# Another head for a fused attention and feed-forward kernel: inputs in another order, the first batch by pairs of tiles, the second from a transposed copy

## The reference

```
xn  = layernorm(x)                              # over the last axis, no gain and no offset
q   = xn @ wq.T + bq;  k = xn @ wk.T + bk;  v = xn @ wv.T + bv
p   = softmax(q @ k.T / 16)                     # 1024 x 1024 for each batch
low = up_aux @ (lora_up @ (lora_down @ down_aux))
out = x + p @ v  +  xn @ (W + low).T + ffn_b
```

## Time and profile before

| What | Value |
|---|---|
| Median of three runs | 518.73 us |
| The profiled execution, its own time | 518.57 us |
| Its span, first to last instruction | 516.8 us |
| Granted TensorE clock over the span | 1.000 |
| PE busy | 506.3 us, 98% of the span |
| DVE, POOL, ACT busy | 367.4, 373.7, 276.6 us |

### The profile page before, as it was taken

How to read it: one execution, slowest core, us unless ns; L and a number is a source line. 1 busy time by engine, 2 the same in 40 slices (tenths; PEclk the granted TensorE clock), 3 DMA queues, 4 the chain that set the end, 5 groups by cost and what they waited for, 6 DMA issues and landing times.

```text
span 516.8 us, 8100 instructions
## 1 busy us (share of the span) xinstructions
PE 506.3 (98%) x2948; PEld 448.6 (87%) x2948; DVE 367.4 (71%) x839; ACT 276.6 (54%) x589; POOL 373.7 (72%) x221
## 2 busy tenths in 40 slices
PE   5999999999999999999999999999999999999997
PEld 4677897989989898898989989898998989899897
DVE  4789866867589584885868767696758748376594
ACT  3746667365744747267381655736474462724450
POOL 2834785986789966999669979699678976671730
PEclk9999999999999999999999999999999999999999
DMA  8020004000040003200050100501002010000001
GB/s 238 39 82 0 1 33 173 1 41 2 26 179 1 41 1 109 96 2 41 1 197 8 42 2 0 204 1 42 0 35 90 1 42 1 41 1 2 41 9 74
DMA packets 8694, 25.04 MB, mean 48 GB/s; under 512 B 1850, under 2 KB 3792, under 8 KB 7760
## 3 DMA queue, kind: packets, MB, share of 16 engines
q1 hardware_dynamic: 7328, 24.38, 13.0%
q10 hardware_dynamic: 1328, 0.16, 0.2%
HBM read 16.15 MB, written 8.39 MB: 47 GB/s over the span
## 4 chain that ended last, share of the span: by engine, by line
PE 94%; DVE 1%; ACT 1%; issue 0%; DVEq 0%
PE o_ps L1078 12%; PE o_ps L1080 12%; PE o_ps L1079 12%; PE g_ps L998 10%; PE g_ps L1000 10%; PE g_ps L999 10%; PE s_ps L998 8%; PE s_ps L999 8%; PE s_ps L1000 8%; PE o_ps L998 1%; PE o_ps L999 1%; PE o_ps L1000 1%; ACT prod L607 1%; PE s_ps L1078 0%; PE s_ps L1080 0%
## 5 line engine op out<-in xcount | busy, mean ns | idle before, releaser
L507 POOL TENSOR_TENSOR p_lo<-s,p_hi 128x1024 fp32r<-128x1024 f32 x60 | 144.3, 2439 | 40.0 <-ACT p_hi L657 40.0
L650 ACT ACTIVATE s<-s,e 128x512 f32<-128x512 f32 x128 | 84.3, 714 | 116.3 <-DVE s L848 116.3
L1078 PE MATMUL o_ps<-v_hi,p_hi 128*128 128x258 f32 x480 | 136.5, 284 | 0.0
L1080 PE MATMUL o_ps<-v_hi,p_lo 128*128 128x258 f32 x480 | 136.0, 283 | 0.0
L1079 PE MATMUL o_ps<-v_lo,p_hi 128*128 128x256 f32 x480 | 135.8, 283 | 0.0
L1079 PEld LDWEIGHTS o_ps<-v_lo,p_hi 128*128 128x128 f32 x480 | 91.5, 191 | 1.6
L1078 PEld LDWEIGHTS o_ps<-v_hi,p_hi 128*128 128x128 f32 x480 | 90.2, 188 | 1.6
L1080 PEld LDWEIGHTS o_ps<-v_hi,p_lo 128*128 128x128 f32 x480 | 91.2, 190 | 0.0
L807 DVE SCALAR_TENSOR_TENSOR tile_max<-s_ps,e,tile_max 128x512 f32<-128x512 f32 x80 | 59.9, 748 | 32.9 <-PE s_ps L1000 30.7
L998 PE MATMUL s_ps<-xt_hi,zt_hi 128*128 128x512 f32 x192 | 75.0, 390 | 0.0
L999 PE MATMUL s_ps<-xt_lo,zt_hi 128*128 128x512 f32 x192 | 74.7, 389 | 0.0
(11 more groups left out here) (157 smaller groups left out, 988.8 us busy)
## 6 DMA issues: line engine op xcount, KB each, us to landing
out<-base SPq DMA_DIRECT2D x15, 512.0 KB, 2.7
x_sb<-in_L_attn_x SPq DMA_DIRECT2D x7, 1024.0 KB, 7.8
x_t<-in_x_t SPq DMA_DIRECT2D x6, 1024.0 KB, 5.8
x_sb<-in_L_attn_x SPq DMA_DIRECT2D x4, 256.0 KB, 6.7
out<-base SPq DMA_DIRECT2D x4, 128.0 KB, 1.9
s<-in_L_attn_wk SPq DMA_DIRECT2D x1, 256.0 KB, 3.1
s<-in_L_attn_wq SPq DMA_DIRECT2D x1, 256.0 KB, 6.2
s<-in_L_attn_wv SPq DMA_DIRECT2D x1, 256.0 KB, 6.9
```

Source lines behind the costliest of these rows:

```text
L507: nc.gpsimd.tensor_tensor(p_pair(g, p_lo_sb, j), s_pair(j), p_pair(g, p_hi_sb, j).bitcast(f32), ALU.subtract).then_inc(p_lo_made, 1)
L650: nc.scalar.activation(s[:, n, :], s[:, n, :], ACT.Exp, bias=e[b % 2][:, n:n + 1]).then_inc(p_made, 1)
L1078: nc.tensor.matmul(o[:, 0:D + ONES], hi, v_hi[i][:, n, 0:D + ONES], start=first, stop=False)
L1080: mm = nc.tensor.matmul(o[:, 0:D + ONES], lo, v_hi[i][:, n, 0:D + ONES], start=False, stop=last)
```

## The change

- Loads: x's first piece goes ahead of wk, wq and wv go ahead of the third and fourth piece. The small columns (bq, bk, lora_down, lora_up) come in one array `small` that the host packs, by one DMA.
- PE order in the head: LoRA, the row for e and the bias columns; then the transposes by pairs of tiles (`turn`), between them A by plain float32 matmuls (`make_a`, no split of wk and wq); then V of the first four tiles (`first_v`, 256 columns), two of z, the other transposes, the first score tile, V of tiles 4 and 5, the second score tile, the other two of z, the other six score tiles, the feed-forward of all tiles (`first_ffn`, 256 columns), and V of tiles 6 and 7.
- Batch 1 uses the transposed copy (`EARLY = 1`): its 16 transposes, `make_xn(1)` and its first `make_prod` go; `load_t(1)`, `make_stat_cols(1)`, two `make_stat_row`, `norm_x_t(1, ...)`, `make_xt_hi` and `make_xt_lo` are added in the head. Its z groups move to places 1 and 2.
- DVE: two of the four `prod` products of batch 0 go from POOL to DVE (`make_late_prod`); `vf_lo` (two subtractions) goes from POOL to DVE; the bn_stats of batch 2 go from the head into the score maxima of chunk 1.

The core of the diff, with the new functions:

```diff
+        TURN_BANKS = (g_ps[0], g_ps[1], g_ps[1], s_ps[3])
+        FIRST_V_BANKS = (o_ps[0], g_ps[0], o_ps[0], o_ps[0])
+        FIRST_Z_BANKS = (s_ps[0], s_ps[1], o_ps[0], o_ps[1])
+        FIRST_FFN_BANKS = (o_ps[0], o_ps[1], o_ps[0], o_ps[1])
...
-        FIRST = [{0: (0, 1), 1: (2, 3), 2: (4, 5), 3: (6, 7)}, V_GROUPS]
-        LATER = [{1: (4, 5), 2: (6, 7)}, V_GROUPS]
+        PLACES = [{1: (0, 1), 2: (2, 3)}, V_GROUPS]
...
             load(1)
+            load_t(1)
             load(2)
...
# POOL
             make_x_bias(0)
...
+            norm_x_t(1, 0)
+            norm_x_t(1, 1)
+            make_xt_lo(1, 0)
             shift_raw(0)
...
# ACT
+            make_raw(0, 1)
             act.wait_ge(ffn_summed, 1)
             nc.scalar.activation(vf_hi[:, :, D:2 * D], ffn_t_sb, ACT.Copy).then_inc(ffn_hi_made, 1)
+            make_stat_cols(1)
+            make_xt_hi(1, 0)
             make_p(0, 0)
             make_p(0, 1)
+            first_v_hi(3)
             make_p_hi(0, 0)
...
             make_p_hi(0, 1)
+            make_xt_hi(1, 1)
             make_p(0, 4)
             make_p(0, 5)
             make_raw(1, 0)
...
# DVE
+            first_z_lo(0)
+            make_late_prod(2)
+            make_late_prod(3)
+            first_z_lo(1)
+            turned_lo(2)
+            turned_lo(3)
...
             nc.vector.tensor_tensor(ffn_t_sb, two(o_ps[1][:, :]), ffn_t_sb, ALU.add).then_inc(ffn_summed, 1)
+            dve.wait_ge(x_loaded[1], DMA)
+            make_stats(1, range(0, 4))
             make_tile_max(0, 0)
+            first_v_lo(2)
+            make_stats(1, range(4, TILES))
+            make_mean_var(1)
             make_tile_max(0, 1)
+            first_z_lo(2)
+            first_z_lo(3)
+            dve.wait_ge(ffn_hi_made, 1)
+            nc.vector.tensor_tensor(vf_lo[:, :, D:2 * D], ffn_t_sb, vf_hi[:, :, D:2 * D].bitcast(f32),
+                                    ALU.subtract).then_inc(ffn_lo_made, 1)
             make_tile_max(0, 2)
             make_tile_max(0, 3)
+            make_stat_row(1, 0)
+            make_tile_max(0, 4)
+            make_stat_row(1, 1)
+            make_tile_max(0, 5)
             nc.vector.tensor_reduce(e_row_sum[:, :], e_row, AXIS, ALU.add).then_inc(e_row_sum_made, 1)
+            make_tile_max(0, 6)
+            make_tile_max(0, 7)
 
             make_max_t(0)
             make_block_max(0)
+            add_first_ffn(0)
             make_max_col(0)
             spread_max_col(0)
+            add_first_ffn(1)
             make_top(0)
             shift(0, 0)
             shift(0, 1)
             shift(0, 2)
+            add_first_ffn(2)
+            shift(0, 3)
...
# PE
+            def first_v(j):
+                pe.wait_ge(turned_lo_made, j + 1)
...
+                elif j == 3:
+                    pe.wait_ge(first_ffn_added, 3)
+                first_tokens(FIRST_V_BANKS[j], j, slice(0, D)).then_inc(first_v_mm, 1)
+
+            def first_ffn(j):
...
+                elif j > 1:
+                    pe.wait_ge(first_ffn_added, j - 1)
+                first_tokens(FIRST_FFN_BANKS[j], j, slice(D, 2 * D)).then_inc(first_ffn_mm, 1)
...
+            pe.wait_ge(small_loaded, DMA)
+            pe.wait_ge(lora_loaded, 2 * DMA)
+            nc.tensor.matmul(o_ps[0][0:RANK, 0:D], lora_down_t, down_aux_sb,
+                             start=True, stop=True).then_inc(low_rank_mm, 1)
             pe.wait_ge(bq_spread, DT)
             pe.wait_ge(wk_loaded, DMA)
...
+            turn(0)
+            make_a(0)
+            turn(1)
+            make_a(1).then_inc(a_mm, 1)
+            first_v(0)
+            first_v(1)
+            first_z(0)
+            first_z(1)
+            turn(2)
+            turn(3)
...
+            scores(0, 0)
+            first_v(2)
+            scores(0, 1)
+            first_z(2)
+            first_z(3)
+            for n in range(2, TILES):
                 scores(0, n)
...
+            for j in range(PAIRS):
+                first_ffn(j)
+            first_v(3)
```

More of the change, by code:

```diff
@@ L274, in two, with pair, group_bank, rstd_count @@
             return ap.rearrange("p (t n) -> p t n", t=DT)
[L276 to L283, removed]
-            return g_ps[k % 2]
[L286 to L296, removed]
+        def pair(ap):
+            return ap.rearrange("p (m n) -> p m n", m=2)
+        TURN_BANKS = (g_ps[0], g_ps[1], g_ps[1], s_ps[3])
+        FIRST_V_BANKS = (o_ps[0], g_ps[0], o_ps[0], o_ps[0])
+        FIRST_Z_BANKS = (s_ps[0], s_ps[1], o_ps[0], o_ps[1])
+        FIRST_FFN_BANKS = (o_ps[0], o_ps[1], o_ps[0], o_ps[1])
+        POOL_PRODS = 2
+        def group_bank(k):
+            return g_ps[k % 2]
+        def rstd_count(b):
+            return len(STAGES) + b
+        def stage_of(tile):
+            return [first <= tile < end for first, end in STAGES].index(True)
+        def prods(b):
+            return PAIRS * b + POOL_PRODS
+        def pair_of_columns(j):
+            return slice(2 * j * PT, (2 * j + 2) * PT)
         LAST = CHUNKS * B - 1
@@ L348, in _, with load_first @@
         def _(sp):
-            sp.dma_start(wk_sb, rows(wk)).then_inc(wk_loaded, DMA)
-            for j in range(4):
+            def load_first(j):
                 n = TILES // 4
@@ L567, in _ @@
         def _(act):
[L568 to L572, removed]
+            act.dma_start(small[:, :], small_in).then_inc(small_loaded, DMA)
@@ new lines, in turned_hi, with first_v_hi, make_z_hi @@
+            def turned_hi(j):
+                act.wait_ge(turned_mm, j + 1)
+                nc.scalar.activation(xt_hi[0][:, :, pair_of_columns(j)], two(TURN_BANKS[j][:, :]), ACT.Copy)\
+                  .then_inc(turned_hi_made, 1)
+            def first_v_hi(j):
+                act.wait_ge(first_v_mm, j + 1)
+                nc.scalar.activation(v_hi[0][:, 2 * j:2 * j + 2, 0:D], pair(FIRST_V_BANKS[j][:, :]), ACT.Copy)\
+                  .then_inc(first_v_hi_made, 1)
+            def make_z_hi(ps, h, d):
+                return nc.scalar.activation(zt_hi[:, d, half(h)], ps[:, :], ACT.Identity, bias=z_bias[:, d:d + 1])
@@ L664, in _ @@
+            make_xn(0)
+            act.wait_ge(wv_loaded, DMA)
+            nc.scalar.activation(vf_hi[:, :, 0:D], wv_t_sb, ACT.Copy).then_inc(wv_hi_made, 1)
+            act.wait_ge(mid_rank_mm, 1)
+            nc.scalar.activation(mid_rank, o_ps[0][0:UDIM, D:2 * D], ACT.Copy).then_inc(mid_rank_made, 1)
+            turned_hi(0)
+            make_xn(2)
+            turned_hi(1)
             act.wait_ge(a_mm, 1)
             nc.scalar.activation(a_hi[:, :, :], two(s_ps[2][:, :]), ACT.Copy, scale=SCALE).then_inc(a_hi_made, 1)
-            for k in range(DT):
-                make_group_hi(0, k)
@@ L893, in _ @@
               .then_inc(b_parts_made, 1)
-            make_first_xn(DVE_XN[1:])
+            dve.wait_ge(wv_hi_made, 1)
+            nc.vector.tensor_tensor(vf_lo[:, :, 0:D], wv_t_sb, vf_hi[:, :, 0:D].bitcast(f32), ALU.subtract)\
+              .then_inc(wv_lo_made, 1)
+            turned_lo(0)
+            make_first_xn(3)
+            for j in range(2, 4):
+                dve.wait_ge(x0_loaded[j], DMA)
+                make_stats(0, range(2 * j, 2 * j + 2))
+            turned_lo(1)
+            make_mean_var(0, range(4, TILES))
             dve.wait_ge(a_hi_made, 1)
@@ L935, in _ @@
[L935 to L939 removed]
+            add_first_ffn(2)
+            shift(0, 3)
+            shift(0, 4)
+            shift(0, 5)
+            add_first_ffn(3)
+            first_v_lo(3)
             for g in range(LAST):
```

490 lines of the change are left out of this document (245 added, 245 removed).

## The result

The changed kernel takes 523.98 us (median of 4, 523.51 to 524.38) against 518.59 in the same measurement: ratio 1.0101, 95% interval 1.0089 to 1.0113, so 5.4 us slower where 4.0 were forecast. The profiled execution took 524.38 us, its span is 522.3, 5.5 more than before.

What follows compares the result with a forecast made beforehand. PE was taken to bound loop and head, DVE's head work to decide the change: +4.7 us at the start of chunk 2's scores, -0.7 for a vanished later wait, so 518.57 + 4.0 = 522.6 us; range 519.2 to 526.0.

Steps and rivals of the forecast that it cites:

- The loads: Start of head: LoRA loads gate PE's first matmul, at 5.1 us; bounds move the end by -0.5 and +2.7.
- The clock: Head: PE's clock rises from 1.2 to 2.4 GHz at 14 us; bounds 9 and 18 move the mark -1.5, +1.9.
- DVE's list: Head, from z_lo(0) to last score maximum: 19.4 us of DVE work plus waits, ending at 43.1; the deciding term.
- Maximum to third add: Behind chunk 0's scores: 7.55 us of dependent DVE work; PE waits 3.0, 0.5, 1.6; chunk 1's scores +4.8.
- Rival 3: PE's gap from 42.5 us: clock falls to the lower level, some 4 us more, 526.6 us; chance 0.07.
- Chunk 1 to the mark: From chunk 1's scores to chunk 2's scores (the mark): P times V at 64.7, mark at 82.2, +4.7 us.
- The wait for raw: Chunk 1's eighth score tile: PE waits for ACT's raw(1, 1), 1.6 us with restart.
- the 0.54 stall: PE's wait for DVE at 86.34 us goes, with its restart: -0.7 us.
- POOL "costs nothing": POOL's added 12.2 us lies in idle time, done at 55 before ACT wants it at 60: no cost.
- Rival 1: Head: DVE keeps up, last maximum before 39.1, PE wins 9.0 us, kernel gets faster, 513.6 us; chance 0.08.

Runs made afterwards that it cites:

- e5: Changed kernel with the two low-rank (LoRA) matmuls moved behind the first transpose pair and A's first half: 522.57 us.
- e10: Changed kernel with 27 matmuls of zeros on PE ahead of the wait for the first loads: 520.02 us.
- e9: e8 and e5 together on the changed kernel: 519.36 us, in two groups, 518.14 to 518.79 and 519.93 to 520.87.
- e13: The kernel of e9 run again unchanged, for a trace: times in the same two groups, profiled execution 520.85 us.
- e7: Changed kernel with the parts of e2, and batch 1's statistics earlier on DVE and ACT: 521.77 us.
- e3: Changed kernel without batch 1's row statistics (16 small ACT instructions, two DVE transposes): 522.2 us.
- e2: Changed kernel with two products of batch 0 and the low part of W moved from DVE to POOL: 523.78 us.
- e8: e7 with V of tiles 6 and 7 ahead of the feed-forward, and the third add behind the fourth shift: 519.87 us.
- e1: Changed kernel with 20 zero-weight matmuls inside the second feed-forward part, so PE does not stand still: 524.53 us.
- e4: Changed kernel with feed-forward parts 0 and 1 between the last score tiles and their adds ahead of the last two maxima: 524.23 us.
- e11: e9 with 22 matmuls of zeros ahead on PE: 515.65 us, ratio 0.9949 to the kernel before.
- e12: Kernel before the change, with 22 matmuls of zeros ahead of its first product: 518.84 us, ratio 1.0005.

## Why the prediction was right, and where it was off

Right in sign, mechanism and range. The time is 1.4 us above the forecast. At the scores of chunk 0 it was 2.7 (26.61, forecast 23.9); the terms behind took 1.3 less than I had summed, so the small miss at the end is in part luck.

- **The loads: mis-sized.** "Between 3.3 and 8.4 I take 5.1" measured 7.47. I priced three small loads by a 1 KB one, although the second 1 KB load of before, bk_col, took 4.5 in the same trace. Here up_aux, 50 KB, is issued at 1.8 and takes 5.51 to land while the 16 DMA engines are full (share 1.04 in the window from 6.2). The Trainium skill (SBUF — State Buffer, The DMA setup-cost knee) gives a fixed 2 us and bytes over a rate, an estimate of 2.1 us for 50 KB; the trace does not agree (5.51). That the large loads beside it make the difference is my reading; no run tests it. e5 takes that wait away: 1.4 us, of which a part is an earlier rise of the clock.
- **The clock: mis-sized.** "I let it rise at 14; bounds 9 and 18" measured about 17.5, within the bounds. Counted from the first matmul it came after some 10 us where I had let 8.9, so most of the 2.7 is the late start. e10 prices all that hangs on it at 4.0 us, and e9 with e13 show that no single value was right: 14.4 and 20.2 for one program. The Trainium skill (TensorE: Matmul & The Clock Gate, Part 1) says that the moment shifts from run to run with where the first matmul falls, by about half a microsecond; the runs agree that it shifts, not with the size.
- **DVE's list: right.** From z_lo(0) to the end of the last maximum I summed 22.05 (21.05 to 43.1); it took 21.4 (23.95 to 45.33), the wait for stat_cols 1.57 against 1.75. e7 and e3 confirm that it decides: 2.2 and 1.8 us. It does not decide alone: the list starts when PE has z, and e10, which only makes PE's head faster, is worth 4.0.
- **Maximum to third add: right.** 7.55 forecast, 7.36 measured (45.33 to 52.69). PE's waits are 2.25 and 0.69, not 3.0, 0.5 and 1.6: PE came to the first one 2.7 later than forecast (45.2), and the slower clock behind it filled the rest (e2, where the clock stayed up, has 2.25, 0.46 and 1.53). e8, where V no longer waits for the third add, gains 1.9.
- **Rival 3 happened and cost nothing.** The clock fell at 48.15 (256-column steps of 0.21 instead of 0.12, back from 51.49). My 4 us assumed that PE would set the end there; DVE's add does (e1, e2).
- **Chunk 1 to the mark.** The wait for raw is 0.81 (1.6 forecast), P times V starts 12.0 behind the scores (12.4), and the 0.54 stall went.
- **POOL "costs nothing": half wrong.** It is done at 54.95, as forecast (55), and ACT does not wait for that. But its list has no slack any more up to 83 us, and a gain on DVE alone is lost to it (e4). It added nothing to the sum, only a second limit beside the first.
- **Rival 1** put its turning point where the last maximum ends before 39.1, with 513.6. e11 reaches 38.55 and 515.65, and e9's shorter execution is level with the kernel before (518.26) at 41.4. So an early last maximum does go with a faster kernel, but both have another order, and no run tests 39.1 in the order of the change. My claim that program order excludes this rival holds only for that order.

What stays open: where in the executions of 518 to 519 us the kernel before with zeros loses what it gains, since there is a clock reading of them but no trace; why the clock stayed up behind the wait of 2.25 in e2; and why its first rise differs by 6 us between executions of one program.

## What to carry to other kernels

When work moves between engines, follow the latest common ancestor of the chains that end together: relieving one (e2, e4) gave nothing (523.78 and 524.23); starting both earlier (e7) and then shortening one (e8) gave 4.1 us. This head of short products ran at half clock for its first 8 to 13 us, so work on TensorE from the first microsecond is worth trying; it took 4.0 us off one order (e10) and nothing off another, in which waits followed (e12). Price a load by one that lands beside the same traffic, not by its size.

## What the runs showed of the hardware

- The first rise of the clock came at 14.4 and at 20.2 us in two executions of one program, whose times differ by 2.6 us (518.26 and 520.85).
- The clock column reads 1.00 in the first stretch at half pace (after, 6.2 to 10.2) and 0.50 to 0.57 only after a fall; in the head the level is read from equal instructions (1.91 against 1.03 us).
- After a wait of 2.25 us the clock fell to half (after, 48.15), but after the same wait in e2 (47.26) it did not. In e12 it fell after waits of 0.82 and 1.85, in e10 at 10.6 after no listed wait.
- A fall that lies in a gap costs nothing where another engine sets the end of the gap: the changed kernel (clock 0.997, 523.98) and e1 (1.000, 524.53) take the same time.
